# A perceiver kernel on one Trainium2 core: the mask of the first cross attention moves into the score matmul, its roots are taken for four contexts at once, its last key becomes a padded block, and its norm and queries are spread over the engines

## What is computed

```
x = x + L0_xattn(_layernorm(x), ctx_1024, mask)      # then eleven more blocks
# L0_xattn(x [64,32,256], mem_seq [64,257,256], mem_mask [64,257]):
xn, mn = _rmsnorm(x, rms_scale), _rmsnorm(mem_seq, rms_scale)
q = einsum('BTD,NDH->BTNH', xn, q_w)                 # 4 heads of 64
k, v = einsum('BSD,cKDH->cBSKH', mn, kv_w)           # one head of 64
q = _apply_rope(q, q_pos) * HEAD_DIM ** (-0.5);  k = _apply_rope(k, k_pos)
masked = where(mem_mask, q . k, -2.3819763e+38)      # [64, 4*32, 257]
enc = softmax(masked) . v
return einsum('BTNH,NHD->BTD', enc, out_w)
```

## Time and profile before

| what | value |
|---|---|
| runs | 4184.21 us median of 3 (4175.63 to 4188.41) |
| profiled execution, its own time | 4177.27 us |
| its span, first to last instruction | 4175.5 us |
| mean granted TensorE clock | 0.922 |
| PE, DVE, ACT, POOL busy | 90%, 53%, 29%, 24% of the span |
| first cross attention in this trace | from 0 to about 403.5 us |

### The profile page before, as it was taken

One profiled execution on the slowest core, in us unless ns is written; L12 is line 12 of the kernel. 1 busy time (PEld: TensorE's weight loads), 2 busy tenths in 40 slices (PEclk: granted clock), 3 DMA queues, 4 the chain that ended last, 5 costly groups with the idle time before them and its releaser, 6 DMA issues.

```text
span 4175.5 us, 91242 instructions
## 1 busy us (share of the span) xinstructions
PE 3745.0 (90%) x38548; PEld 2810.8 (67%) x38548; DVE 2196.4 (53%) x5609; ACT 1200.5 (29%) x3052; POOL 987.7 (24%) x1588
## 2 busy tenths in 40 slices
PE   7988873799899598999999989999999999999996
PEld 5666552655577477777787755676777867777774
DVE  5555663325445635555655546555444456665346
ACT  3343320123111021333333334323222234443111
POOL 4776722302100033322222223220000010002002
PEclk7776975999999599999999999999999999999997
DMA  3331013637100121111111110003112111111000
GB/s 129 97 106 59 3 34 128 221 101 229 42 2 3 58 65 48 51 47 43 50 47 46 33 49 2 2 3 108 61 61 71 56 50 37 39 38 56 2 2 24
DMA packets 197766, 240.31 MB, mean 58 GB/s; under 512 B 17812, under 2 KB 179088, under 8 KB 194288
## 3 DMA queue, kind: packets, MB, share of 16 engines
q1 hardware_dynamic: 191408, 203.02, 15.6%
q0 software_dynamic: 5952, 31.46, 2.2%
HBM read 221.51 MB, written 12.64 MB: 56 GB/s over the span
## 4 chain that ended last, share of the span: by engine, by line
PE 67%; DVE 11%; issue 7%; POOL 3%; ACT 2%; DMA 1%; SPq 0%; ACTq 0%; POOLq 0%; DVEq 0%
PE psum L180 44%; PE psum L3168 9%; PE psum L762 2%; DVE l3x_P L3500 2%; PE psum L734 1%; PE psum L2604 1%; PE psum L3396 1%; PE psum L2705 1%; PE psum L2673 1%; DVE l3x_V L3483 1%; PE psum L747 1%; DVE g_xn L243 1%; PE psum L219 1%; PE psum L2614 1%; POOL l0a_ms L946 1%
## 5 line engine op out<-in xcount | busy, mean ns | idle before, releaser
L230 POOL TENSOR_SCALAR g_rs<-g_mv 128x4 f32<-128x4 f32 x44 | 18.0, 410 | 1082.4 <-DVE g_mv L278 1081.2
L3168 PE MATMUL psum<-l2f_hhi,l2f_whi 128*128 128x512 f32 x512 | 200.8, 392 | 0.0
L3168 PE MATMUL psum<-l2f_hlo,l2f_whi 128*128 128x512 f32 x512 | 199.2, 389 | 0.0
L3168 PE MATMUL psum<-l2f_hhi,l2f_wlo 128*128 128x512 f32 x512 | 199.2, 389 | 0.0
L180 PE MATMUL psum<-l2x_kT,l2x_Qp 128*128 128x257 f32 x768 | 177.5, 380 | 2.6 <-ACT g_xn L3064 2.6
L180 PE MATMUL psum<-g_xn,l2x_tok 128*128 128x384 f32 x512 | 177.7, 489 | 1.4 <-ACT g_xn L3073 1.4
L289 DVE TENSOR_TENSOR g_x<-g_x,psum 128x256 f32<-128x256 f32 x144 | 59.9, 417 | 181.8 <-PE psum L180 179.5
L180 PEld LDWEIGHTS psum<-l2x_kT,l2x_Qp 128*128 128x128 f32 x768 | 140.8, 190 | 21.2 <-issue 3.0
L3214 DVE CAST l2f_hhi<-l2f_tmp 128x512 fp32r<-128x512 f32 x96 | 41.0, 427 | 202.0 <-ACT l2f_tmp L3272 200.9
L180 PE MATMUL psum<-l0x_wkv,l0x_ctxT 128*128 128x128 f32 x512 | 103.7, 368 | 34.8 <-ACT l0x_kv L639 34.5
L219 PE MATMUL psum<-g_ident,g_xn 128*128 128x128 f32 x352 | 77.6, 369 | 63.7 <-DVE g_xn L243 62.1
(11 more groups left out here) (733 smaller groups left out, 9715.8 us busy)
## 6 DMA issues: line engine op xcount, KB each, us to landing
l2f_raw<-L2f_h SPq DMA_DIRECT2D x64, 512.0 KB, 3.5
l0x_ctxT<-ctxT SPq DMA_DIRECT2D x64, 257.0 KB, 3.0
l1x_ctxT<-ctxT SPq DMA_DIRECT2D x64, 257.0 KB, 5.7
l0x_ctok<-ctx SPq DMA_DIRECT2D x64, 256.0 KB, 2.7
l1x_ctok<-ctx SPq DMA_DIRECT2D x64, 256.0 KB
l2x_cT<-ctxT SPq DMA_DIRECT2D x64, 256.0 KB, 2.7
l2x_tok<-ctx SPq DMA_DIRECT2D x128, 128.0 KB, 2.8
l3x_ctxT<-ctxT SPq DMA_DIRECT2D x64, 256.0 KB, 2.7
```

Of the source, the lines that this page charges most:

```text
L3168: t = e.matmul(z, a, b, start=c == 0 and u == 0, stop=c == 7 and u == 2)
```

## The change

Only `l0_xattn` and the layout of its mask input change; the eleven later blocks stay. Per part:

- **Mask as a 65th row.** `qT` and `kT` get a 65th row: ones in `qT`, the mask's bias of the context in `kT` (a row of `mbias`, made once on POOL for all contexts, and copied to `kT[64]` by one DMA of 257 floats per context). The score matmul then has 65 rows and adds the bias. POOL's `mask` per context is gone, the mask's DMA shrinks from 2 MB to 16 KB, `kT` gets a fourth buffer.
- **Softmax.** DVE takes the negated row maximum straight from PSUM (one reduction), ACT's exponential reads the scores from PSUM, and the reciprocal becomes a stage `divide` of its own with lag 7.
- **Roots of four contexts.** `root` works on a 128x8 tile, once in four ticks. `stats` runs three ticks further ahead (`ahead`), and SP loads `ctok` further ahead, on its own semaphores.
- **Last key as a padded block.** `P` is 384 wide with zeros behind column 257, `vt1` has 128 rows of which 127 are zero: the third transpose and the third product of `values` have full size, and ACT copies `PT` in one piece. Transposed probabilities have one bank instead of two, the outputs two instead of one.
- **Scaling the outputs** is split: DVE two heads, ACT two heads (new in the loop).
- **Order.** DVE's is [6, 7, 8, 1, 10], ACT's [9, 2, 4, 6, 7, 8], POOL's [2, 1], PE's stays.
- **Norm and queries.** x arrives and is normalized group by group, ACT applies the norm and evicts, the addition at the end of the rotary goes from DVE to POOL, the rotary has three buffers, and the tail, the statistics of contexts 0 to 3 and the first root are done inside the query loop.

```
-        kT, mb = [T(f"kT{k}", [64, 257]) for k in range(3)], [T(f"mb{k}", [128, 257]) for k in range(3)]
-        P, PT = [T(f"P{k}", [128, 257]) for k in range(2)], [T(f"PT{k}", [128, 384]) for k in range(2)]
+        kT = [T(f"kT{k}", [65, 257]) for k in range(4)]
+        P, PT = [T(f"P{k}", [128, 384]) for k in range(2)], [T(f"PT{k}", [128, 384]) for k in range(2)]
...
+            def mask_row(b):
+                if b >= 4:
+                    w.wait_ge(s_ps.at(b - 3))
+                load(e, row[b % 4], kT[b % 4][64:65, :], mbias[b:b + 1, :])
...
             def turn_p(b):
...
-                e.transpose(z[:, 0:128], P[b % 2][:, 0:128], ident[:])
-                e.transpose(z[:, 128:256], P[b % 2][:, 128:256], ident[:])
-                e.transpose(z[0:1, 256:384], P[b % 2][:, 256:257], ident[:]).then_inc(*p_turn.up())
+                for kt in range(3):
+                    t = e.transpose(bank[4][:, 128 * kt:128 * kt + 128], P[b % 2][:, 128 * kt:128 * kt + 128], ident[:])
+                t.then_inc(*p_turn.up())
...
+            def root(g):
+
+                w.wait_ge(stat.at(4 * g + 4))
+                r, m = rr[:, 4 * g:4 * g + 4, :], mvc[:, 4 * g:4 * g + 4, :, :]
+                e.tensor_tensor(r, m[:, :, :, 0], m[:, :, :, 0], ALU.mult).then_inc(*pstep.up())
...
+            for i in range(16):
+                w.wait_ge(q_mul.at(i + 1))
+                e.tensor_tensor(rA[i % 3][:], rA[i % 3][:], rB[i % 3][:], ALU.add).then_inc(*q_rot.up())
+                if i == 3:
+                    w.wait_ge(masks.at(1))
+                    e.tensor_scalar(mbias[:], mi[:].bitcast(U8)[:, 0:257], 1.0, FILL, ALU.subtract, ALU.mult).then_inc(*mb_ok.up())
+                if i == 9:
+                    root(0)
...
+            ticks(64, {1: roots, 2: rotate}, [2, 1])
...
             def soft(b):
                 w.wait_ge(s_ps.at(b + 1))
-                w.wait_ge(mb_ok.at(b + 1))
-                if b >= 2:
-                    w.wait_ge(p_turn.at(b - 1))
-                e.tensor_tensor_reduce(out=P[b % 2][:], in0=bank[2 + b % 2][:, 0:257], in1=mb[b % 3][:], scale=1.0,
-                                       scalar=LOWEST, op0=ALU.add, op1=ALU.max, accum_out=sm[:, b, 0:1]).then_inc(*s_ok.up())
-                w.wait_ge(s_ok.now())
-                e.tensor_scalar(sm[:, b, 1:2], sm[:, b, 0:1], -1.0, None, ALU.mult).then_inc(*top.up())
+                e.tensor_reduce(sm[:, b, 1:2], bank[2 + b % 2][:, 0:257], AX.X, ALU.max, negate=True).then_inc(*top.up())
+
+            def divide(b):
                 w.wait_ge(exps.at(b + 1))
                 e.reciprocal(sm[:, b, 3:4], sm[:, b, 2:3]).then_inc(*sums.up())
...
-            ticks(64, {1: stats, 6: soft, 8: scale, 10: total}, order)
+            ticks(64, {1: ahead, 6: soft, 7: divide, 8: scale, 10: total}, [6, 7, 8, 1, 10])
...
             def probsT(b):
-                z = bank[4 + b % 2]
                 w.wait_ge(p_turn.at(b + 1))
                 if b >= 2:
                     w.wait_ge(o_ps.at(b - 1))
-                copy_act(e, PT[b % 2][:, 0:256], z[:, 0:256])
-                copy_act(e, PT[b % 2][0:1, 256:384], z[0:1, 256:384]).then_inc(*PT_ok.up())
+                copy_act(e, PT[b % 2][:], bank[4][:, 0:384]).then_inc(*PT_ok.up())
...
-            ticks(64, {2: keys, 4: keysT, 6: power, 7: probsT, 9: outT}, order)
+            ticks(64, {2: keys, 4: keysT, 6: power, 7: probsT, 8: scale, 9: outT}, [9, 2, 4, 6, 7, 8])
```

More of the change, by code:

```diff
@@ new lines, in sp, with fetch_tok @@
+            for g in range(2, 4):
+                load(e, xin[g], x[:, 4 * g:4 * g + 4, :], xsrc[:, 4 * g:4 * g + 4, :])
+            load(e, misc, rope_q[:], A["rope_q"])
+            load(e, misc, rope_t[:], A["rope_t"])
+            load(e, masks, mi[:], A["mask"])
+            def fetch_tok(b):
+                if b >= 4:
+                    w.wait_ge(stat.at(b - 3))
+                load(e, tok[b % 4], ctok[b % 4][:], A["ctx"][b, 0:256, :].rearrange("(k p) d -> p k d", p=128))
+                mark["tok", b] = tok[b % 4].now()
@@ L370, in sp @@
+                mark["ctx", b] = full[b % 4].now()
+            def mask_row(b):
+                if b >= 4:
+                    w.wait_ge(s_ps.at(b - 3))
+                load(e, row[b % 4], kT[b % 4][64:65, :], mbias[b:b + 1, :])
+                mark["row", b] = row[b % 4].now()
+            for b in range(4):
+                fetch_tok(b)
+            load(e, rope_in, rope_k[:], A["rope_k"])
+            load_rows(e, wo_in, wo, A["L0x_o"])
             for b in range(4):
                 fetch(b)
+            w.wait_ge(const.at(1))
@@ L372, in sp @@
+            load(e, onerow, qT[64:65].rearrange("a i j h q -> a (i j h q)"), ones[0:64, :])
+            w.wait_ge(mb_ok.at(1))
+            for b in range(4):
+                mask_row(b)
+            w.wait_ge(zeros.at(3))
             w.wait_ge(t_v.at(1))
-            load(e, vrow, vt1[:], vt[:])
+            load(e, vrow, vt1[0:1], vt[:])
+            for b in range(4, 8):
+                fetch_tok(b)
             for b in range(4, 64):
                 fetch(b)
+                if b + 4 < 64:
+                    fetch_tok(b + 4)
+                if b >= 8:
+                    mask_row(b - 4)
@@ L377, in pe @@
+            for b in range(60, 64):
+                mask_row(b)
         def pe(e):
@@ L379, in pe, with freed, take @@
             w.wait_ge(ident_ok.at(1))
-            norm.pe(e, w)
-            w.wait_ge(mark["w"])
-            norm.all_ready(w)
             banks = Banks(bank[0:4])
-            def q_freed(key):
+            def freed(key):
                 what, i = key
-                w.wait_ge(q_rot.at(i + 1) if what == "q" else qT_ok.at(i + 1))
+                w.wait_ge({"q": q_mul, "t": qT_ok}[what].at(i + 1) if what != "tail" else (t_v.at(2), kTt_ok.at(1))[i])
+            def take(key):
+                z, prev = banks.take(key)
+                if prev:
+                    freed(prev)
+                return z
@@ L389, in q1, with turn_x @@
+            def turn_x(g):
+                if g >= 2:
+                    w.wait_ge(xT_ok.at(2 * g - 2))
+                for c in range(2):
+                    for i in range(4 * g, 4 * g + 4):
+                        w.wait_ge(x_n.at(i + 1))
+                        t = e.transpose(norm_bank(g, c)[:, (i % 4) * 128:(i % 4 + 1) * 128], xn[:, i, c * 128:(c + 1) * 128],
+                                        ident[:])
+                    t.then_inc(*n_turn.up())
             def q1(i):
-                z, prev = banks.take(("q", i))
@@ L524, in rotate, with roots @@
                 e.tensor_tensor(kr[k][:], kr[k][:], kr2[k][:], ALU.add).then_inc(*kr_ok.up())
[L526 to L533 removed]
+            def roots(b):
+                if b % 4 == 3 and b + 4 < 64:
+                    root((b + 4) // 4)
@@ L535, in dve, with x_stats @@
+            ticks(64, {1: roots, 2: rotate}, [2, 1])
         def dve(e):
             w = K.w(e)
+            st = K.st
+            def x_stats(g):
+                w.wait_ge(xin[g].at(1))
+                for i in range(4 * g, 4 * g + 5):
+                    if i < 4 * g + 4:
+                        e.bn_stats(st[:, i, :], x[:, i, :]).then_inc(*dstep.up())
+                    if i > 4 * g:
+                        w.wait_ge(dstep.back(1 if i < 4 * g + 4 else 0))
+                        e.bn_aggr(mv[:, i - 1, :], st[:, i - 1, :]).then_inc(*xstat.up())
@@ L575, in dve @@
[L575 to L583 removed]
+                e.tensor_tensor(b[:, :, 32:64], v[:, :, 0:32], sq[:, :, 32:64], ALU.mult).then_inc(*q_mul.up())
@@ L630, in act @@
             e.activation(tmp[:, 0, :], z[0:64, 0:64], ACT.Copy, scale=mvt[:, 3:4]).then_inc(*t_v.up())
+            evict(1)
+            normed(2)
+            evict(2)
+            normed(3)
+            for i in range(16):
+                turned(i)
+                if i == 2:
+                    evict(3)
             w.wait_ge(kTt_ok.at(1))
```

280 lines of the change are left out of this document (160 added, 120 removed).

## The result

The changed kernel takes 4022.91 us (median of 4 runs, 4012.24 to 4024.19), the kernel before beside it 4186.31 us (4175.63 to 4191.33): a ratio of 0.9607, interval 0.9582 to 0.9633. The profiled execution took 4023.51 us with a span of 4021.8 us, so the span is 153.7 us shorter. The medians give 163; in a later comparison, where the kernel before had 4172.88, they gave 149.

A forecast was written before the change was run, and what follows sets the result against it. POOL was taken to bound the context loop at the high clock, PE at the low. Head 47, fill 14, loop 180, drain 15 and low clock 12 make 268 us instead of 403.5, hence 4049 us, range 4022 to 4108.

The forecast's parts named there:

- the 268 of the sum: First cross attention: the predicted end of the block, 268 us instead of 403.5, 135.5 us less.
- the allowance for a low clock: Start of the context loop: stalls of head and fill may leave the clock low, 5 ticks at 2.4 us more, 12 us.
- PE's tick: Context loop, high clock: ticks back to back, a plain one 2.6 to 2.95 us, 3.1 us per context.
- POOL is the bound: Context loop before, high clock: POOL's nine instructions and gaps fill the 4.41 us period, busy for 3.92.
- the statistics, hence the roots, stand behind it: Context loop before: DVE's reciprocal waits 68.1 us for the same tick's exponential, with statistics and roots behind; no separate price.
- So the stalls cost twice: Context loop before: stalls cost directly and by the clock, which is low in the stretches that follow them.
- Head, fill, drain: Around the context loop: keys start at 47 us instead of 52.7, fill 14 instead of 22.8, drain 15 instead of 26.
- The other engines: Context loop, work per context: POOL 2.2 us, ACT 2.6 (2.8 with pauses), DVE 2.2 to 2.4.
- B: Context loop: the clock stays low for a third to a half of it, 4093 to 4124 us; 16%.
- C: Context loop: a ring of waits through ACT's copy of turned probabilities replaces POOL, 4.0 us a tick, 4095 us; 8%.
- D: Context loop: the clock stays low throughout, 6.15 us per context, slower at 4232 us; 4%.
- E: Context loop: no gain, something unseen such as a late mask row in every tick holds the old period; 2%.

The follow-up runs named there:

- before_mask3: The kernel before with the mask's bias made for the first three contexts only and reused for the others; 4172.30 us, ratio 0.9977.
- pool2: The changed kernel with two idle fills of 128x1024 on POOL after each context's rotation; 4107.20 us, ratio 0.9834 to the kernel before.
- pool_old: The changed kernel with idle fills of 1024, 1024 and 512 columns on POOL after each rotation; 4138.67 us, ratio 0.9912 to the kernel before.
- before_both: The kernel before with DVE's statistics one tick earlier and the mask's bias made for the first three contexts only; 4101.67 us, ratio 0.9799.
- gap5: The changed kernel with five fills on POOL after the queries, for which PE waits before its first keys; 4033.96 us, ratio 0.9663 to the kernel before.
- best: The changed kernel with PE projecting and turning outputs later, ACT copying them last, the query blocks' addition back on DVE; 4015.07 us, ratio 0.9623.
- pe_old: The changed kernel with 64 rows in the scores and the last key as one row again; 4051.37 us, ratio 0.9712 to the kernel before.
- late_o: The changed kernel with PE turning the outputs after the keys' transposition and ACT copying them last; 4019.26 us, ratio 0.9639 to the kernel before.

## Where the prediction failed, and where it was right

The measured time lies 2 us below the prediction's range. The block ends 20 us before the 268 of the sum, and two of its terms failed: the allowance for a low clock, 12 us that weren't there, and PE's tick, 11 us too long over the loop. That the miss falls just outside the range and not just inside is luck: by the two profiled executions alone, 153.8 us apart, the time would be 4184.2 - 153.8 = 4030, inside.

*What bounded the kernel: right, and incomplete.* "POOL is the bound" holds for the periods at the high clock: 4.40 us without a wait. POOL's work put back costs 115 of the 155 us. What the prediction didn't see is the ring right below it, 4.37 us, which before_mask3 lays bare: 1.1 us off POOL there was answered by 18 us more of waiting for the statistics, and 47 us for ACT's copy. The prediction had the statistics in one clause ("the statistics, hence the roots, stand behind it") and gave them no price; their price was 36 us alone, and more together with POOL's work. The sum survived because the change removed both at once and I counted the new period from PE, not from what was taken away.

*"So the stalls cost twice": right, and it hangs on that same wait.* pool2 and pool_old bring the alternating clock back, and before_both takes it away. In the kernel before the low clock holds PE's tick, and through the statistics POOL, for up to the 44.2 us of waits. With the statistics ahead POOL goes on meanwhile, and PE catches up at the high clock: there a low clock costs at most the 7 and 9 us that POOL's ticks leave unexplained in pool2 and pool_old.

*PE's tick: failed, by its size.* The prediction had 2.6 to 2.95 us for the plain tick and 3.1 per context; measured were 2.50 and 2.91, 11 us less over 58 contexts. It took the idle weight loads of the earlier trace rows for a sign of any change in the number of rows and so left open whether 65 would help; they go with 64 rows and stay away with 65. The one row was priced at 0.1 to 0.15 us and takes 0.28, since it also costs ahead of the product and at the transposition; the 64 rows take 0.31 of the "up to 0.35 more, or nothing". Against it, turning and projecting cost 0.43 per context instead of 0.27, because in these ticks PE waited for ACT's scaling and, behind ACT's copy of the outputs, for kT. The Trainium skill, TensorEngine Tiling (Array Packing), counts a contract dimension of up to 64 as row tiling (When to Use Tiling) and says that a change of the mode drains the engine (Key Properties). The runs agree as far as they show it: 65 rows avoid the cost, and 64 instead of 65 cost 9.6 us over the block, where I had put 12. That the engine drains is in no row; the idle weight loads are.

*The allowance for a low clock: failed, there was none.* "I count 5 ticks at 2.4 us more, 12 us." The clock didn't fall ahead of the drain. In the kernel before it fell inside the wait at the tail of the keys, and the change takes that wait away; gap5, with a pause twice as long, brings the low clock back and pays 6.7 us for it. I had seen the tail move in the part on the head and did not draw the consequence for the clock.

*Head, fill, drain: right within 4 us.* Keys start at 48.68 (47 predicted), the fill takes 11.9 us (14), the drain 18.6 (15). A query block takes 1.64 us (1.65) where nothing comes between. *The other engines* too: per context POOL takes 2.04 us (2.2), ACT 2.55 (2.6), DVE 2.16 (2.2 to 2.4). The addition on POOL costs less than the 3 us counted: best's head is 0.6 to 1.3 us shorter. The Trainium skill, GPSIMD Engine Reference, 4.1 Engine selection, would have it on VectorE; that is right here by about a microsecond.

The errors add up to -12.0 (allowance), -11.4 (ticks), -2.1 (fill), +1.7 (head) and +3.6 (drain): 20.2 us less than the 268 of the sum, 247.8. The remaining 9 us to the ratio's 4019.8 are 11 in the medians, which differ by up to 13 us for the kernel before between comparisons, less the 1.6 that the later blocks give back. Of the rivals, B, C, D and E did not come; ACT, feared in C, is idle 13% of the loop.

A path through the runs shows where the 155 us came from: before 403, statistics ahead 367, and less mask work 328, the roots by fours with the changed head and ACT's and VectorE's parts 275 (pe_old), the operands 248. That 328 to 275 hides a head 4 us shorter and no low clock up to 85 us: by the first addition to x pe_old is 17 of the 53 us ahead (82.45 against 99.87), and it gains the other 35 after that, at 3.36 us a context in the loop against 3.86. I did not part them further.

## What to carry to other kernels

When an engine looks like the bound, look at what ends its idle time too: if that is work of the same tick, taking work off it gives little until the other is done a tick earlier, and here that was one number in the order. Look at such waits at each level of the clock by itself: here they stood only where it was low. Price a low clock by who has to wait for the slow tick: 44 us of waits where the other engine was tied to it, under 10 where that engine could work ahead. And ask of each change which pause ahead of a busy stretch it removes. A wait that is moved within a tick comes back elsewhere until the consumer is moved as well (late_o against best).
